# Scores of the causal and gated attention layers from rounded parts in fp32r, and the second sequence's causal layer moved beside the first biased layer

## The chip, the cores and the metric

The kernel runs on one core of a Trainium2 chip. The time is the device time of one execution in microseconds (us), the median of several runs. The engines are TensorE (PE for its matmuls, PEld for its weight loads), VectorE (DVE), ScalarE (ACT), GpSimd (POOL) and SyncE (SP), which here issues the DMAs.

## What is computed

Eight sequences of 512 tokens and 256 features go through four layers, each a layer norm, an attention and a sum with the input. The causal layer (0) and the gated layers (1 and 3) have 16 heads of 16 features; the biased layer (2) has 16 heads of 64.

```python
x = x + attn_a(_layernorm(x), ...)   # causal: rope on Q and K, softmax(QK/4), triangle
x = x + ffn(_layernorm(x), ...)      # gated: the 256 tokens with the highest gate attend to each other
x = x + attn_b(_layernorm(x), ...)   # biased: relative bias added to the scores
x = x + ffn(_layernorm(x), ...)      # gated again
```

All of it is float32, and the selection by the gate's order means that small errors could swap tokens.

## The kernel before

The work is cut into steps, such as `c_p1` or `b_row`, each of which belongs to one sequence and one layer. The letters are c for causal, f for gated and b for biased. `whole()` lists the steps with what each needs and follows, `in_order()` puts them in one order by a table of numbers `PLACE` (with the costs `WORK` as the planner's view of when banks come free), and every engine then walks its part of this one order. Engines meet by semaphores. The 8 banks of PSUM are given out by the planner in the same order.

Biased layers follow one another in the order of sequences and make up the main line. Beside biased layer s run the gated layer 3 of sequence s-1, the causal layer of sequence s+1 and the gated layer 1 of sequence s+1, one after the other, since they share one stretch of memory (`side[0]`). One such round is called a cycle here. Causal layer 1 is an exception: it has a second stretch (`side[1]`, which the biased layers use later), runs together with causal layer 0 and gated layer 1 of sequence 0, and biased layer 0 waits for it.

The scores of the small heads are computed twice. Pass 1 (`c_p1`, `f_p1`) gives queries by keys, from which DVE takes each row's maximum. The maxima are turned by PE (`c_m`, `f_m`). Pass 2 (`c_p2`, `f_p2`) gives keys by queries with the maximum subtracted, ACT takes the exponential, and the result is the operand for the values (`c_va`, `c_vb`, `f_va`, `f_vb`). Four heads are handled at once, one in each quarter of PE's 128 rows: 32 rows per matmul, 16 of which carry the head. Of the other 16, one holds ones in K (`K1`, `K1f`) and, before pass 2, the maximum in Q (`Qz`, `Qzf`), so that the maximum is subtracted by the same matmul. A causal layer has four such groups of four heads (`n` = 0 to 3), each in three steps per pass (`q` = 0: tiles 0 and 1 in pass 1; 1: tile 2; 2: tile 3), with 1280 columns per head and pass. A gated layer has four groups, one step per pass, with 512 columns.

All these operands are fp32. The trace records an fp32 matmul as two matmul records, each with its weight load. An fp32r matmul (`pick` by `xn_hi`, `xn_lo` in the gather) has one record. Where PE would be idle for long by the planner's view, transposes of `ident` fill the place (L1341).

## Time and profile before

| | |
|---|---|
| time, median of 3 runs | 2104.51 us (2104.4 to 2105.33) |
| the profiled execution | 2105.06 us |
| its span in the trace | 2103.3 us |
| PE busy in the span | 97% |
| DVE, ACT, POOL busy | 70%, 53%, 29% |

The span is the time from the first to the last instruction in the trace; 1.8 us of the profiled execution lie around it. Busy shares are means over the whole program, so a start in which engines wait for each other is mixed with the long even part.

### The profile page before, as it was taken

What the parts mean: (1) busy time and instruction counts of PE and PEld (TensorE: products, weight loads), DVE (VectorE), ACT (ScalarE), POOL (GpSimd) and SP (SyncE); (2) the same over time, 40 slices, a digit from 0 to 9 for tenths busy, and PEclk for the clock granted to TensorE, in tenths of its full rate; (3) what the DMA queues carried; (4) which work ended last, traced back from release to release, by engine and by line L of the source; (5) the groups of instructions that cost most, each with busy time, mean ns of one, the idle gap of its engine ahead of it and who ended that gap; (6) DMA issues with size and microseconds to landing.
All of it is one profiled execution on the core that took longest, in us unless ns stands there. A gap on an engine that the chain in (4) does not pass through costs nothing.

```text
span 2103.3 us, 38722 instructions
## 1 busy us (share of the span) xinstructions
PE 2029.9 (97%) x14644; PEld 1243.3 (59%) x14644; DVE 1467.4 (70%) x4578; ACT 1110.2 (53%) x2497; POOL 600.8 (29%) x817
## 2 busy tenths in 40 slices
PE   7889999999999999999999999999999999999997
PEld 4456556655665555765566645666456654666565
DVE  8887654777757766678767687576875777866435
ACT  1444664746537474464734646365563656535642
POOL 4212132243222342233411423124231243212220
PEclk9999999999999999999999999999999999999998
DMA  3001121121111110111101111012100121111200
GB/s 143 2 1 41 43 76 58 50 81 34 44 41 57 57 44 26 48 67 48 42 21 58 58 47 44 18 59 71 46 31 27 51 73 49 44 34 51 76 3 11
DMA packets 29047, 98.56 MB, mean 47 GB/s; under 512 B 2880, under 2 KB 11200, under 8 KB 28736
## 3 DMA queue, kind: packets, MB, share of 16 engines
q1 hardware_dynamic: 28864, 96.09, 13.6%
q8 instruction: 118, 1.93, 0.4%
q14 instruction: 65, 0.53, 0.1%
HBM read 91.89 MB, written 4.19 MB: 46 GB/s over the span
## 4 chain that ended last, share of the span: by engine, by line
PE 85%; DVE 7%; ACT 6%; issue 1%; POOL 0%; DMA 0%; SPq 0%; DVEq 0%; ACTq 0%; POOLq 0%
PE ps L861 26%; PE ps L1532 11%; PE ps L1550 10%; PE ps L1322 9%; PE ps L1540 9%; PE ps L1379 4%; PE ps L1488 3%; PE ps L1399 3%; PE ps L1500 3%; PE ps L1469 3%; PE ps L1413 2%; ACT PTc L1057 2%; ACT PT L1097 2%; DVE ps L1176 2%; DVE mcol L1251 1%; ACT probs L1088 1%
## 5 line engine op out<-in xcount | busy, mean ns | idle before, releaser
L1015 POOL TENSOR_SCALAR probs<-probs,rtotal 128x512 f32<-128x512 f32 x512 | 344.9, 693 | 871.8 <-DVE rtotal L1277 871.3
L1088 ACT ACTIVATE probs<-probs,peak 128x512 f32<-128x512 f32 x512 | 365.0, 714 | 220.9 <-DVE peak L1273 220.9
L1268 DVE CUSTOM_DVE_ANT_0 probs<-ps,band 128x512 f32<-128x512 f32 x512 | 332.6, 687 | 107.8 <-PE ps L1532 106.4
L1097 ACT ACTIVATE PT<-ps 128x512 f32<-128x512 f32 x512 | 263.1, 619 | 78.1 <-PE ps L1540 77.9
L1176 DVE CUSTOM_DVE_ANT_0 ps<-ps,later 128x128 f32<-128x128 f32 (+3 forms) x512 | 233.3, 525 | 40.9 <-PE ps L1379 40.0
L1540 PEld LDWEIGHTS ps<-ident,probs 128*128 128x128 f32 x2048 | 223.3, 141 | 52.0 <-issue 43.3
L1532 PE MATMUL ps<-KT,QT 64*128 64x512 f32 x1024 | 252.4, 611 | 0.0
L1540 PE MATMUL ps<-ident,probs 128*128 128x128 f32 x2048 | 248.3, 275 | 0.1
L1550 PE MATMUL ps<-PT,Vb 128*64 128x512 f32 x1024 | 235.9, 600 | 0.1
L861 PE MATMUL ps<-xnT,wb 128*128 128x512 f32 x512 | 233.0, 598 | 1.3 <-ACT PT L1097 0.7
L1057 ACT ACTIVATE PTc<-ps 128x384 f32<-128x384 f32 (+1 forms) x384 | 167.7, 542 | 64.8 <-PE ps L1399 64.7
L1251 DVE TENSOR_REDUCE mcol<-ps 128x2 f32<-128x512 f32 x256 | 157.3, 683 | 14.8 <-PE ps L1469 14.0
L1068 ACT ACTIVATE PTf<-ps 128x512 f32<-128x512 f32 x256 | 131.7, 604 | 63.0 <-PE ps L1488 62.6
L861 PEld LDWEIGHTS ps<-xnT,wb 128*128 128x128 f32 x512 | 92.9, 190 | 102.0 <-issue 96.8
L1532 PEld LDWEIGHTS ps<-KT,QT 64*128 64x128 f32 x1024 | 94.5, 186 | 92.9 <-issue 67.9
L1550 PEld LDWEIGHTS ps<-PT,Vb 128*64 128x64 f32 x1024 | 67.1, 137 | 139.2 <-issue 121.8
L861 PEld LDWEIGHTS ps<-wb,xnT 128*128 128x128 f32 x1024 | 122.6, 192 | 26.5 <-issue 16.7
L1007 POOL TENSOR_SCALAR_AFFINE_SELECT PTc<-PTc 128x512 f32<-128x512 f32 x128 | 82.1, 654 | 178.0 <-ACT PTc L1057 177.3
L983 POOL TENSOR_TENSOR rstd<-veps,pow_half 128x2 f32<-128x2 f32 x64 | 47.0, 737 | 280.8 <-DVE veps L1118 280.8
L861 PE MATMUL ps<-wb,xnT 128*128 128x128 f32 x1024 | 125.7, 276 | 0.0
L1322 PE MATMUL ps<-wob,OTb 128*128 128x256 f32 x512 | 114.0, 380 | 0.8 <-DVE OTb L1279 0.8
L1379 PE MATMUL ps<-K,Qz 32*128 32x128 f32 (+3 forms) x1024 | 96.5, 471 | 14.8 <-ACT PTc L1057 4.9
(133 smaller groups left out, 2887.3 us busy)
## 6 DMA issues: line engine op xcount, KB each, us to landing
band<-in_band SPq DMA_DIRECT2D x64, 896.0 KB, 4.6
wb<-in_w_b SPq DMA_DIRECT2D x64, 384.0 KB, 3.0
x<-in_x SPq DMA_DIRECT2D x16, 256.0 KB, 2.9
out<-x SPq DMA_DIRECT2D x16, 256.0 KB, 2.2
wob<-in_wo_b SPq DMA_DIRECT2D x1, 1024.0 KB, 8.7
wqk<-in_wqk_a SPq DMA_DIRECT2D x1, 512.0 KB, 6.2
cos_t<-in_cos SPq DMA_DIRECT2D x1, 256.0 KB, 5.4
sin_t<-in_sin SPq DMA_DIRECT2D x1, 256.0 KB, 6.5
```

Source lines behind the costliest of these rows:

```text
L861: last = nc.tensor.matmul(o, w, r, start=(i == 0), stop=(i == len(pairs) - 1))
L1015: last = g.tensor_scalar(unit, unit, rtotal[:, r % 8, e:e + 1], 1.0, ALU.mult, ALU.mult)
L1057: a.activation(pt_c(m, q)[:, h], bank(now, name)[:, 0:w], ACT.Exp).then_inc(act_read, 1)
L1088: last = a.activation(unit, unit, ACT.Exp, bias=peak[:, r % 8, e:e + 1], accum_out=total[:, r % 8, e:e + 1])
L1097: a.activation(PT[:, k % 2, e, :, tile_of(q)], bank(now, name).rearrange("p (k n) -> p k n", k=NT), ACT.Copy).then_inc(act_read, 1)
L1176: last = v.tensor_tensor_reduce(out=scores, in0=scores, in1=later[:, NT * P - w:NT * P], scale=1.0, scalar=-3e38, op0=ALU.add, op1=ALU.max ...
L1268: v.tensor_tensor_reduce(out=probs[:, r % ROWS_HELD, e, :], in0=bank(now, name), in1=band[:, k % 2, e, lo:lo + T], scale=1.0, scalar=-3e38 ...
L1322: last = te.matmul(o[:, j * D:(j + 1) * D], w, r, start=(k == 0 and j == 0), stop=(k == count - 1 and j == 1))
L1379: last = te.matmul(o[h][:, at_:at_ + w], m.Qz[group(h), c, e, tile_of(t)], m.K1[group(h), c, e, 0:w], start=True, stop=True)
L1532: full(te.matmul(bank(now, name), QT2[half(e), k % 2, tile_of(q)], KT2[half(e), k % 2, :], start=True, stop=True), now, name)
L1540: last = te.transpose(bank(now, name)[:, tile_of(t)], probs[:, r % ROWS_HELD, e, tile_of(t)], ident[:])
L1550: last = te.matmul(o[half(e), :], Vb[:, k % 3, q, half(e)], PT[:, k % 2, e, q, :], start=(q == 0), stop=(q == NT - 1))
```

## The change

The scores come from rounded fp32r parts. K is copied to both halves of the 32 rows and split into `HI` (rounded) and `LO` (the rest). Q is copied to both halves too, and `X` holds the rounded Q in one half and the rest in the other. `X` times `LO` plus `X` times `HI` is then the whole product of Q and K in two fp32r matmuls in place of one fp32 matmul. In pass 2 a third fp32r matmul subtracts the maximum: `M` (the turned maxima, themselves split in two by `c_hm` and `f_hm`) by `sel`. The scale 1/4 moves into the exponential. New steps make the parts: `c_dq`, `c_rq`, `c_xq`, `c_dk`, `c_hk` in a causal layer, `f_rq`, `f_xq`, `f_hk` in a gated one. They take the place of `c_hq` and the old `c_hk`, and `c_m`, `f_m` lose their DVE part to a copy on ACT.

The memory of the parts leaves no second stretch for a causal layer, so causal layer 1 follows gated layer 1 of sequence 0 and uses `side[0]`. The table `PLACE` and the costs `WORK` are new throughout.

```diff
@@ causal_steps, ffn_steps
-        out += [(c("q", i), [c("xt")], []), (c("k", i), [c("xt")], []), (c("hq", i), [c("q", i)], []),
-                (c("hk", i), [c("k", i)], [])]
+        out += [(c("q", i), [c("xt")], []), (c("k", i), [c("xt")], []), (c("dq", i), [c("q", i)], []),
+                (c("rq", i), [c("dq", i)], []), (c("xq", i), [c("rq", i)], []), (c("dk", i), [c("k", i)], []),
+                (c("hk", i), [c("dk", i)], [])]
+    out += [(f("rq"), [f("q")], []), (f("xq"), [f("rq")], []), (f("hk"), [f("k")], [])]
@@ whole
-    causal = [add(causal_steps(s), [], []) for s in range(2)]
-    entered = [add(ffn_steps(0, 1), causal[0], [])]
-    side = add(ffn_steps(1, 1), causal[1], entered[0])
+    entered = [add(ffn_steps(0, 1), add(causal_steps(0), [], []), [])]
+    side = add(ffn_steps(1, 1), add(causal_steps(1), [], entered[0]), [])
...
-        if s == 0:
-            layer = [(x, a, b + causal[1] * (x.kind == "b_k" and x.n == 0)) for x, a, b in layer]
@@ POOL
+                        if kind in ("c_hk", "f_hk"):
...
+                                last = g.tensor_tensor(low, both, high, ALU.subtract)
@@ ACT
+                        if kind == "c_rq":
...
+                            for e in range(2):
+                                last = a.activation(m.X[:, n, e], m.Dq[:, n, e], ACT.Copy, scale=sides[:, 0:1])
+                        if kind in ("c_m", "f_m"):
...
+                            a.activation(parts, bank(now) if kind == "c_m" else bank(now)[:, 0:CAP],
+                        if kind == "c_hk":
...
+                                a.activation(m.HI[:, n, e], m.LOf[:, n, e], ACT.Copy).then_inc(high_k_done, 1)
@@ DVE
+                        if kind in ("c_dq", "c_dk"):
...
+                                last = v.stream_shuffle(pairs[:, n, e], turned, [DH * e + r % DH for r in range(32)])
+                        if kind in ("c_xq", "f_xq"):
...
+                                last = v.scalar_tensor_tensor(out=parts, in0=both, scalar=sides[:, 1:2], in1=parts,
-                        if kind in ("c_m", "f_m"):
...
-                                last = v.scalar_tensor_tensor(out=rows[e], in0=peaks, scalar=sides[:, 6 + e:7 + e],
@@ PE, c_p1 (f_p1 alike)
-                                for h in range(4):
-                                    last = te.matmul(o[h][:, at_:at_ + w], m.Qz[group(h), c, e, tile_of(t)],
-                                                     m.K1[group(h), c, e, 0:w], start=True, stop=True)
+                                for some in (m.LO, m.HI):
+                                    for h in range(4):
+                                        last = te.matmul(o[h][:, at_:at_ + w], m.X[group(h), c, e, tile_of(t)],
+                                                         some[group(h), c, e, 0:w], start=(some is m.LO), stop=(some is m.HI))
@@ PE, c_p2 (f_p2 alike)
+                                for i in range(3):
+                                    for h in range(4):
+                                        one = sel[group(h), e:e + 1].to_broadcast([32, P])
+                                        w_ = (m.LO[group(h), c, e, tile_of(t)], m.HI[group(h), c, e, tile_of(t)], one)[i]
+                                        r_ = m.M[c][group(h), t * P:T] if i == 2 else m.X[group(h), c, e, t * P:T]
```

Of the table a line or two, as it stands everywhere:

```diff
-CYCLE = 2805
+CYCLE = 24741
-    ("cycle", "c_p1"): [-6358, 1818, 1797, -1735, 1672, 1720, 1843, 1993, 2033, 2063, 2084, 2140],
```

What this does to the order is seen on PE at the start of the program. Before, the second sequence's transposes of `xn` and its projections (`xnTc_103`) stand between the first sequence's projections (`xnTc_99`) and scores (`Qz_96`, `K_97`):

```order
L1341 MATMUL ps<-ident 128x128 x6
L861 MATMUL ps<-xnTc_99,wqk 128x512 x6
L1352 MATMUL ps<-ident,xn 128x128 x8
L861 MATMUL ps<-xnTc_99,wqk 128x512 x2
L861 MATMUL ps<-xnTc_103,wqk 128x512 x2
L1379 MATMUL ps<-K_97,Qz_96 128x128 x4
L1379 MATMUL ps<-K_97,Qz_96 128x256 x4
L861 MATMUL ps<-wva,xnTc_103 128x256 x4
```

Now only one sequence is at work there, all its projections come first, and transposes of `ident` fill the place before its scores:

```order
L1455 MATMUL ps<-ident 128x128 x6
L940 MATMUL ps<-xnTc_108,wqk 128x512 x8
L940 MATMUL ps<-wva,xnTc_108 128x256 x8
L1455 MATMUL ps<-ident 128x128 x29
L1494 MATMUL ps<-LO_102,X_98 128x128 x4
L1494 MATMUL ps<-HI_100,X_98 128x128 x4
L1494 MATMUL ps<-LO_102,X_98 128x256 x4
L1494 MATMUL ps<-HI_100,X_98 128x256 x4
```

Each block of four score matmuls has become two. The other place is PE where biased layer 0 begins (`xnT,wb` are its projections, `KT,QT` its scores). Before, gated layer 1 of sequence 1 starts beside it (`gate_80`), its causal layer having ended just ahead (`woa,Qz_100`):

```order
L1322 MATMUL ps<-woa,Qz_100 128x256 x8
L1341 MATMUL ps<-ident 128x128 x13
L1352 MATMUL ps<-ident,xn 128x128 x8
L1341 MATMUL ps<-ident 128x128 x6
L861 MATMUL ps<-xnT,wb 128x512 x6
L861 MATMUL ps<-wb,xnT 128x128 x8
L1426 MATMUL ps<-ident,gate_80 128x128 x4
```

Now the causal layer of sequence 1 begins here (the second transposes of `xn`, then `xnTc_108,wqk`) and its scores stand among the biased ones:

```order
L1466 MATMUL ps<-ident,xn 128x128 x8
L940 MATMUL ps<-xnTc_108,wqk 128x512 x8
L940 MATMUL ps<-xnT,wb 128x512 x4
L940 MATMUL ps<-wb,xnT 128x128 x8
L940 MATMUL ps<-xnT,wb 128x512 x4
L940 MATMUL ps<-wb,xnT 128x128 x8
L940 MATMUL ps<-wva,xnTc_108 128x256 x4
L1656 MATMUL ps<-KT_89,QT_88 128x512 x12
L940 MATMUL ps<-xnT,wb 128x512 x4
L940 MATMUL ps<-wb,xnT 128x128 x8
L1494 MATMUL ps<-LO_102,X_98 128x128 x4
```

The whole causal layer of sequence 1 has moved past the start of biased layer 0. The third place is DVE in the first gated layer. Before, K's parts are made in one step from PSUM (the ISA rows are a row maximum and its result):

```order
L1176 ISA ps,mcol_104<-ps,later 128x256
L1176 ISA mcol_104 128x1
L1240 TENSOR_SCALAR K1f_107<-ps,sides 128x512 x2
L1176 ISA ps,mcol_104<-ps,later 128x512
L1176 ISA mcol_104 128x1
```

Now DVE copies K (`gLOf`) and Q (`gDq`), and finishes `gX` after ACT has rounded it:

```order
L1354 TENSOR_SCALAR spread_t_126<-ps,slot_col 128x512 x2
L1281 STREAM_SHUFFLE gLOf_112<-ps 128x512 x2
L1281 STREAM_SHUFFLE gDq_114<-ps 128x512 x2
L1358 COPY Vx<-ps 128x32x16
L1275 SCALAR_TENSOR_TENSOR gX_109<-gDq_114,sides,gX_109 128x512 x2
L1365 TENSOR_REDUCE peaks<-ps 128x2 x8
```

No maxima of the other causal layer stand between these rows now. Counted over the whole order, PE changes its shape of tile (whole array, quarters of rows, halves, quarters of columns) 740 times before and 767 times now, and the transposes of `ident` between the gated layer and the next biased layer (x6 in each cycle) are gone.

## Rows read from the trace of the kernel before

**Rows 1.** The page, by engine: busy us, share of the span, instructions.

```profile
PE 2029.9 (97%) x14644; PEld 1243.3 (59%) x14644; DVE 1467.4 (70%) x4578; ACT 1110.2 (53%) x2497; POOL 600.8 (29%) x817
```

**Rows 2.** Windows, one cycle: length, busy us by engine (instructions), clock, DMA share, GB/s.

```profile
1094.92:1348.13 253.21, 249.08 (x1807) 151.24 (x1806) 182.34 (x572) 138.91 (x312) 74.56 (x100) 1.00 0.14 47
```

**Rows 3.** PE timeline, output projections of biased layers 6, 7: start us, length us.

```profile
1854.37 0.81 PE L1322 MATMUL ps<-wob,OTb 128*128 128x256 f32 x3
...
2032.66 1.56 PE L1322 MATMUL ps<-wob,OTb 128*128 128x256 f32 x6 [0.79 <-DVE OTb L1279]
```

**Rows 4.** PE timeline around 1005 us, columns as in rows 3.

```profile
1003.70 0.93 PE L1379 MATMUL ps<-K,Qz 32*128 32x384 f32 x8
1004.56 1.97 PE L1540 MATMUL ps<-ident,probs 128*128 128x128 f32 x16
1006.62 1.14 PE L1379 MATMUL ps<-K,Qz 32*128 32x512 f32 x8
1007.69 2.84 PE L1540 MATMUL ps<-ident,probs 128*128 128x128 f32 x24
1010.46 0.94 PE L1399 MATMUL ps<-Qz,K 32*128 32x256 f32 x16
```

**Rows 5.** PE timeline, the gather of the first gated layer (fp32r).

```profile
113.40 0.28 PE L861 MATMUL ps<-pick,xn_hi 128*128 128x256 f32 x1
...
114.95 0.28 PE L861 MATMUL ps<-pick,xn_lo 128*128 128x256 f32 x1
```

**Rows 6.** Weight-load timeline, two score steps of rows 4.

```profile
1006.59 0.34 PEld L1379 LDWEIGHTS ps<-K,Qz 32*128 32x128 f32 x8 [0.30 <-ACT PT L1097]
...
1010.46 0.74 PEld L1399 LDWEIGHTS ps<-Qz,K 32*128 32x128 f32 x16 [0.17 <-ACT PT L1097]
```

**Rows 7.** Groups on PE in the cycle of rows 2: busy us, mean ns.

```profile
L1399 PE MATMUL ps<-Qz,K 32*128 32x512 f32 (+3 forms) x128 | 11.9, 463 | 1.3 <-ACT PTc L1057 1.0
L1379 PE MATMUL ps<-K,Qz 32*128 32x256 f32 (+3 forms) x128 | 11.8, 463 | 0.4 <-DVE mcol L1176 0.3
L1413 PE MATMUL ps<-PTc,Vx 128*32 128x512 f32 (+3 forms) x128 | 10.5, 439 | 0.0
...
L861 PE MATMUL ps<-xnTc,wqk 128*128 128x512 f32 x16 | 7.3, 599 | 0.4 <-ACT xnTc L1040 0.4
...
L861 PE MATMUL ps<-wva,xnTc 128*128 128x256 f32 x16 | 3.9, 386 | 0.0
...
L1322 PE MATMUL ps<-woa,Qz 128*128 128x256 f32 x16 | 3.7, 386 | 0.0
```

**Rows 8.** PE timeline of the start of the program.

```profile
91.25 3.72 PE L1322 MATMUL ps<-woa,Qz 128*128 128x256 f32 x16 [0.55 <-DVE Qz L1206]
...
105.38 0.65 PE L1426 MATMUL ps<-ident,gate 128*128 128x128 f32 x4 [2.69 <-DVE gate L1211]
...
170.28 0.50 PE L1322 MATMUL ps<-of_hi,spread_t 128*128 128x256 f32 x2 [0.61 <-DVE of_lo L1282]
...
179.15 1.13 PE L861 MATMUL ps<-xnT,wb 128*128 128x512 f32 x2 [0.30 <-ACT xnT L1040]
```

**Rows 9.** PE timeline of the last gated layer.

```profile
2046.58 3.98 PE L1341 MATMUL ps<-ident 128*128 128x128 f32 x35
2052.48 0.65 PE L1426 MATMUL ps<-ident,gate 128*128 128x128 f32 x4 [1.92 <-DVE gate L1211]
...
2097.57 0.51 PE L1322 MATMUL ps<-of_hi,spread_t 128*128 128x256 f32 x2 [0.61 <-DVE of_lo L1282]
```

**Rows 10.** Groups by shape over the program: busy us, mean ns of one.

```profile
L993 POOL TENSOR_TENSOR xn_lo<-xn,xn_hi 128x512 fp32r<-128x512 f32 x32 | 40.1, 1275 | 62.1 <-ACT xn_hi L1033 62.1
...
L1184 DVE SCALAR_TENSOR_TENSOR Qz<-ps,sides,Qz 128x512 f32<-128x512 f32 x32 | 22.4, 741 | 0.9 <-PE ps L1389 0.9
...
L1159 DVE STREAM_SHUFFLE K<-ps 128x512 f32<-128x512 f32 x16 | 11.8, 736 | 0.0
...
L1033 ACT ACTIVATE xn_hi<-xn 128x512 fp32r<-128x512 f32 x32 | 18.2, 614 | 0.0
```

750 lines of the change are left out of this document (429 added, 321 removed).

## The prediction

> **What bounds the kernel now.** I read the page first, for which engine could bind. TensorE (PE) is busy in 97% of the span, the next engine in 70% [rows 1]. Then the PE timeline for the period: between the output projections of successive biased layers lie 253.2 us, and in one such cycle PE is busy 249.1 of 253.2 us at full clock, DVE 182.3, ACT 138.9, POOL 74.6 [rows 2]. So in six cycles PE's queue sets the time, and PE work taken out there is worth its length as long as the others keep up. From projection 6 to 7 it takes 178.3 us [rows 3], without a causal layer and one of the two gated ones: causal plus gated are worth 74.9 us of PE. The start is different. The first biased projection runs at 179.15 us [rows 8], and ahead of it PE waits for maxima, exponentials and gates. There, removing PE work is worth nothing and the length of the chain counts. The end (last gated layer alone) is such a chain too [rows 9].
>
> **PE, the scores, before.** Two pass-1 steps alone between other work: the 384-column one takes 0.86 us to the next start, the 512-column one 1.07 [rows 4]. The difference is 0.21 us for 128 columns, 1.65 ns a column, and what is left over is 0.22 us for the change of tile shape. A group of four heads has 1280 columns in each pass: 2.11 us of streaming. A gated group has 512 columns a pass: 0.845 us.
>
> **PE, the scores, after.** The trace has fp32r matmuls, on the whole array: from one of 256 columns to the next, 13 matmuls take 1.55 us, 0.12 us each, with their weight loads [rows 5]. That is 0.47 ns a column. An exact quarter of fp32's 1.65 would be 0.41, which I take as the other end. A matmul of 128 columns can't come faster than its weight load: transposes of 128 columns come each 0.115 us (24 in 2.77 us) [rows 4], so I take 0.11 as floor for a block of four quarters. At 0.47:
> - pass 1 of a causal group: 2 x (0.11 + 0.12) + 2 x 0.18 + 2 x 0.24 = 1.30 in place of 2.11;
> - pass 2, three matmuls for one: 0.72 + 0.54 + 3 x (0.11 + 0.12) = 1.95 in place of 2.11;
> - gated: 4 x 0.12 = 0.48 and 6 x 0.12 = 0.72 in place of 0.845 each.
>
> With four groups a layer that saves 3.9 us per causal and 2.0 per gated layer. At 0.41 (and 0.11 for 256 columns too) it is 5.2 and 2.4. I take 4.6 and 2.2, nearer the middle, since four small blocks may hide some of the gap between matmuls. The changes of shape stay (740 before, 767 now): 27 more at about 0.11 us, 3 us.
>
> The Trainium skill (TensorE: Matmul & The Clock Gate, LDWEIGHTS) gives a load 107 ns for 128 columns whatever the rows, which the trace's 0.115 us bears out. It also says there that a load overlaps running matmuls only in other row groups; I weigh that under the rivals.
>
> **The other engines.** Causal layer: DVE gains 8 shuffles and 4 sums at 0.74 us and loses 4 sums for the maxima and 4 scalings of K of about the same length: +3 us. Gated: 4 shuffles and 2 sums in, 2 scalings and 4 half-length sums out: +1.5. POOL gains 4 subtractions of 1.275 us per causal and 2 per gated layer: +5.1 and +2.6. ACT gains four roundings at 0.61 and two copies per causal layer, +3.7, and 2 per gated layer [rows 10]. Per cycle DVE goes to 188, ACT to 147, POOL to 85 us, in a cycle of 244: 77%, 60%, 35% [rows 2]. They cost nothing there, with PE's 95% or more as cover. In a chain that nothing covers they cost: in the gated layer alone, Q now takes shuffles 1.5, ACT 1.3, DVE 1.4, against 1.3 on ACT only: +3 us.
>
> **The sequence moved: the start.** Causal layer 0's output projection starts at 91.25 us [rows 8]. I leave that: DVE no longer serves the other sequence, but the maxima of one sequence and then ACT's exponentials of the last two groups stay in series, and Q and K get longer. From there the gated layer ran mixed with causal layer 1. Alone, its price is in the tail: 5.9 us from the end of the biased projection to the gate's transposes (2046.6 to 2052.5), then 45.1 to the last projection (2097.6) [rows 9]. So: 91.25 + 3.7 (the projection [rows 8]) + 5.9 + 45.1 + 3 = 149.0, and then the 8.9 us which lie between this projection and the biased layer now (170.28 to 179.15 [rows 8]): 157.9. The start ends 21 us sooner.
>
> But the causal layer that filled it is still to be done, and now stands in PE's queue beside biased layer 0, where PE is full. Its PE work in a cycle: 11.9 + 11.8 + 10.5 + 7.3 + 3.9 + 3.7 [rows 7] and about 2.4 of transposes, 51.5 us. These busy times overlap by some 5%; I take 49. What covered it before was idle PE; that cover is gone.
>
> **The sum**, on the profiled span of 2103.3: start -21; causal layer 1 moved +49; score matmuls in PE-bound stretches, 7 causal layers x 4.6 and 14 gated x 2.2 (all but sequence 0's causal and first gated and the very last gated): -63; changes of shape +3; the last gated layer's longer chain +3; the cycle's six filling transposes (0.8 us, six times) -5. Together -34: 2069. The three runs' median lies 0.6 below the profiled execution, and 1.8 us lie around the span: 2070 us, 1.6% faster. The cycle becomes 253.2 - 4.6 - 4.4 - 0.8 + 0.4 = 243.8.
>
> **Rivals.**
> 1. *Quarter-array weight loads set the pace (slower).* Blocks of 27 to 30 ns per pair of load and matmul are what I assume. The loads of 8 pairs begin within 0.34 us less one load of 0.185, 22 ns apart, but those of 16 pairs 37 ns apart [rows 6], there perhaps held by streaming. Per pair at 37 ns: a causal group 0.59 + 0.32 + 0.43 + 0.64 + 0.48 + 0.89 = 3.35, saving 0.9; a gated one 1.48, saving 0.2. Then -63 becomes -38 and the time 2096. At 54 ns (16 pairs in the 0.86 us of a step) pass 2 costs more than before and the time is 2160. It decides at 39 ns: no gain. By the Trainium skill (the same section), load and stream in one row group would add up and the new steps would be slower than the old ones; the gather speaks against it, with 0.12 us for both in the same rows [rows 5]. Chance 0.12.
> 2. *The side chain sets the cycle.* Gated, causal and gated layer follow one another in `side[0]` in each cycle. Unmixed they take 56.7 (the tail from 2046.6 to the end), 95 and 56.7: 208 us. With the longer Q and K about 220 of a cycle of 244. DVE's queue mixes the biased layer's maxima into it, so 24 us of slack may not do. Price: each microsecond that the cycle keeps costs 6. At a cycle of 247 the time is 2089, at 249.3 it is no change, at 253 slower by 1% (2125). For it: PE still waited in each cycle and had six filling transposes; against it: these are gone from the new order. Chance 0.16, a third of it beyond no change.
> 3. *More is gained.* The even stretch loses its waits (4.1 us of a cycle [rows 2]) and streaming is 0.41: cycle 240, time 2045. Chance 0.1.
> 4. *The start doesn't shorten.* Alone, the first sequence leaves PE at half clock and everything waits. Then +15: 2085. It is within the forecast's range; I count it there.
>
> **How the numbers follow.** The forecast (2055 to 2088) has 0.62, more by rival 3 0.10, rival 1 0.12 (half of it beyond no change), rival 2 0.16. The range reaches down to rival 3 and up to the milder ends of rivals 1 and 2: 2043 to 2103. Within 0.2% (4 us) is about what a measurement can't tell from no change. Faster: 0.62 + 0.10 + 0.05 + 0.09 = 0.86 less a little for what I don't see, 0.84. Same: 0.05. Slower: 0.11.
>
> **What would show it in the changed kernel's profile.** The starts of output projections of biased layers 2 to 6 should be 244 us apart; over 249 means rival 2 or 1. Pass-1 steps of 512 columns alone should take 0.70 us to the next start, gated pass-2 steps about 0.95; if 1.3, rival 1. The first biased projection should start near 158 us. DVE should be busy about 75% of the span, and PE still 96% or more. If PE's share falls to 94% with DVE or ACT as releasers, rival 2 has happened. The prediction is wrong if the start takes as long as before, or if the cycle's fall isn't the sum of its score steps' fall.

## The result

The changed kernel takes 2112.95 us (median of 6 runs, 2106.36 to 2113.5), the kernel before 2103.77 beside it: the ratio is 1.0036, with a 95% interval of 1.0026 to 1.0047. The forecast was 2070 us and faster; the kernel is slower by 0.4%. The profiled execution took 2113.5 us, with a span of 2111.8.

The page of the changed kernel by engine, the granted clock of TensorE over the span in 40 slices, and the chain that ended last:

```profile
PE 1989.5 (94%) x15710; PEld 1264.7 (60%) x15710; DVE 1543.4 (73%) x4834; ACT 1162.5 (55%) x2610; POOL 688.6 (33%) x879
...
PEclk7889999999999999999999999999999999999998
...
PE 65%; DVE 22%; ACT 6%; POOL 3%; issue 2%; DVEq 0%
```

TensorE works 40 us less than in [rows 1], and the span is 8 us longer. Its share is 94%, not 96. The chain runs over DVE for 22% of the span, where it was 7% before.

The windows between the starts of the output projections of biased layers 0 to 6, columns as in [rows 2]; the last line sums the six:

```profile
356.95:606.85 249.90, 240.90 (x1930) 151.84 (x1929) 192.33 (x604) 145.21 (x326) 85.86 (x108) 0.99 0.15 48
606.85:858.91 252.06, 242.66 (x1929) 151.56 (x1928) 192.47 (x604) 145.27 (x326) 85.79 (x108) 0.99 0.14 47
...
sum 1507.72, PE 1453.52 PEld 912.05 DVE 1154.56 ACT 872.00 POOL 515.06; mean PE 242.25 PEld 152.01 DVE 192.43 ACT 145.33 POOL 85.84
```

The cycle is 251.3 us on average, where 243.8 was forecast and [rows 2] has 253.2. Two things are to be seen. TensorE is busy 242.25 us of it, 9.0 less than the cycle, while in [rows 2] it is 4.1 less. And the clock is 0.99. Every cycle before had 1.00.

The chain of waits, TensorE's own, in the same six cycles (us in total, times, longest):

```profile
PE ps L1494 <- DVE peaks L1291: 13.2, 18, 1.3
PE ps L1589 <- DVE Vx L1358: 9.3, 6, 1.5
PE ps L940 <- DVE above L1340: 7.9, 6, 1.3
PE ps L1494 <- DVE X L1275: 6.5, 12, 0.9
PE ps L1518 <- ACT PTc L1163: 3.2, 12, 0.3
```

L1494 and L1589 are the first passes over the scores, causal and gated. TensorE's waits come to 8.6 us per cycle on the timeline (3.1 before), and most of the new ones end with DVE by the profile.

One of them has nothing to do with the added instructions. Before the comparisons `above` of a gated layer, GpSimd subtracts `xn_lo`; neither is new. In the kernel before GpSimd was done when they began. GpSimd first, then DVE:

```profile
1301.65 2.51 POOL L993 TENSOR_TENSOR xn_lo<-xn,xn_hi 128x512 fp32r<-128x512 f32 x2 [4.21 <-ACT xn_hi L1033]
```

```profile
1305.55 0.34 DVE L1221 TENSOR_SCALAR above<-gate_row,gate 128x256 bf16<-128x256 f32 x1
```

In the changed kernel they meet, and a comparison of 256 columns takes 1.37 us in place of 0.34:

```profile
1314.62 2.66 POOL L1068 TENSOR_TENSOR xn_lo<-xn,xn_hi 128x512 fp32r<-128x512 f32 x2 [6.39 <-ACT xn_hi L1117]
```

```profile
1314.78 1.37 DVE L1340 TENSOR_SCALAR above<-gate_row,gate 128x256 bf16<-128x256 f32 x1
1316.07 1.36 DVE L1343 TENSOR_SCALAR above<-gate_row,gate 128x256 bf16<-128x256 f32 x1
```

Two comparisons in each of the six cycles are so long, and the wait behind them, 1.31 us each time, makes the 7.9 us of L940. Every run below with the changed kernel's order in the cycle has it unchanged, also those with less side work. No run removes it alone.

One of the waits put down to the maxima, on TensorE's timeline (start, length, tile, wait ahead of it):

```profile
503.19 0.41 PE L1518 MATMUL ps<-M,sel 32*128 32x512 f32 x4
504.91 0.45 PE L1494 MATMUL ps<-LO,X 32*128 32x384 f32 x4 [1.31 <-DVE peaks L1291]
505.16 0.37 PE L1494 MATMUL ps<-HI,X 32*128 32x384 f32 x4
505.46 1.09 PE L1664 MATMUL ps<-ident,probs 128*128 128x128 f32 x8
506.81 0.59 PE L1518 MATMUL ps<-X,LO 32*128 32x384 f32 x4 [0.26 <-ACT PT L1199]
507.14 0.59 PE L1518 MATMUL ps<-X,HI 32*128 32x384 f32 x4
507.46 0.59 PE L1518 MATMUL ps<-M,sel 32*128 32x384 f32 x4
507.96 0.48 PE L1494 MATMUL ps<-LO,X 32*128 32x128 f32 x4
```

and the granted clock there, by windows of TensorE alone:

```profile
502.00:505.00 3.00, 1.60 (x32) 1.00 0.41 131
505.00:506.00 1.00, 1.00 (x13) 1.00 0.00 0
506.00:507.00 1.00, 0.74 (x10) 0.98 0.00 0
507.00:508.00 1.00, 1.00 (x16) 0.50 0.00 0
508.00:509.00 1.00, 1.00 (x19) 0.50 0.07 16
509.00:510.00 1.00, 1.00 (x8) 0.50 0.00 0
```

TensorE waits 1.31 us ahead of 504.91, and from 507 to 510 the clock is 0.50, the lower of its two levels (1.2 GHz). The blocks of 384 columns show it: 0.59 us long and 0.32 between starts at 507.14, and 0.37 long at 505.16, still at full clock. The clock shows 11 such stretches (half-clock stretches from here on) in the six cycles, none before. Each costs about 1.6 us. All 11 begin within 2.1 us of the end of a wait of 1.3 or 1.5 us. But of the 18 waits of that length in the six cycles 7 are not followed by one, with the same instructions around them. The place of 504.91 three cycles later, and the clock behind it:

```profile
1258.11 0.45 PE L1494 MATMUL ps<-LO,X 32*128 32x384 f32 x4 [1.31 <-DVE peaks L1291]
```

```profile
1260.00:1262.00 2.00, 1.64 (x29) 1.00 0.00 0
```

So the wait comes first, and what decides whether the clock falls after it isn't shown.

The first pass of a gated layer, columns the same:

```profile
909.98 0.32 PE L1589 MATMUL ps<-gHI,gX 32*128 32x256 f32 x4
910.09 0.32 PE L1589 MATMUL ps<-gLO,gX 32*128 32x256 f32 x4
910.21 0.32 PE L1589 MATMUL ps<-gHI,gX 32*128 32x256 f32 x4
912.07 0.39 PE L1589 MATMUL ps<-gLO,gX 32*128 32x256 f32 x4 [1.54 <-DVE Vx L1358]
```

Four matmuls of 256 columns come every 0.11 to 0.12 us, as in [rows 5]. Then comes a wait of 1.54 us.

### The profile page after: what moved, and what is told of

It is laid out like the page before. It is cut to its first block, busy times and chain, and to the rows that moved or that the text cites. A ratio compares the mean times of both kernels' runs of the same rounds, so it can differ in the third digit from the quotient of the medians.

```text
span 2111.8 us, 41452 instructions
## 1 busy us (share of the span) xinstructions
PE 1989.5 (94%) x15710; PEld 1264.7 (60%) x15710; DVE 1543.4 (73%) x4834; ACT 1162.5 (55%) x2610; POOL 688.6 (33%) x879
## 4 chain that ended last, share of the span: by engine, by line
PE 65%; DVE 22%; ACT 6%; POOL 3%; issue 2%; DVEq 0%
PE ps L940 17%; PE ps L1436 9%; PE ps L1664 9%; PE ps L1674 8%; PE ps L1656 8%; DVE ps L1291 5%; DVE probs L1382 5%; PE ps L1518 3%; PE ps L1623 2%; ACT PTc L1163 2%; PE ps L1611 2%; PE ps L1532 2%; PE ps L1494 2%; PE ps L1589 2%; DVE peaks L1365 1%
## 5 line engine op out<-in xcount | busy, mean ns | idle before, releaser
L1099 POOL TENSOR_SCALAR probs<-probs,rtotal 128x512 f32<-128x512 f32 x512 | 352.0, 708 | 516.8 <-DVE rtotal L1391 516.7
L1664 PE MATMUL ps<-ident,probs 128*128 128x128 f32 x2048 | 253.1, 277 | 0.6
L1664 PEld LDWEIGHTS ps<-ident,probs 128*128 128x128 f32 x2048 | 227.7, 142 | 40.3 <-issue 30.3
L1291 DVE CUSTOM_DVE_ANT_0 ps<-ps,later 128x512 f32<-128x512 f32 (+3 forms) x512 | 233.4, 526 | 21.9 <-PE ps L1494 21.5
L940 PE MATMUL ps<-xnT,wb 128*128 128x512 f32 x512 | 238.8, 611 | 0.8 <-DVE peak L1382 0.5
L1365 DVE TENSOR_REDUCE peaks<-ps 128x2 f32<-128x512 f32 x256 | 157.0, 683 | 19.2 <-PE ps L1589 19.2
L940 PEld LDWEIGHTS ps<-xnT,wb 128*128 128x128 f32 x512 | 94.8, 192 | 117.3 <-issue 111.7
L940 PEld LDWEIGHTS ps<-wb,xnT 128*128 128x128 f32 x1024 | 121.8, 192 | 16.8 <-issue 10.4
L940 PE MATMUL ps<-wb,xnT 128*128 128x128 f32 x1024 | 127.1, 278 | 0.3
L1436 PEld LDWEIGHTS ps<-wob,OTb 128*128 128x128 f32 x512 | 96.2, 190 | 12.5
```

The costliest lines, as they stand in the source:

```text
L940: last = nc.tensor.matmul(o, w, r, start=(i == 0), stop=(i == len(pairs) - 1))
L1099: last = g.tensor_scalar(unit, unit, rtotal[:, r % 8, e:e + 1], 1.0, ALU.mult, ALU.mult)
L1291: last = v.tensor_tensor_reduce(out=scores, in0=scores, in1=later[:, NT * P - w:NT * P], scale=1.0, scalar=-3e38, op0=ALU.add, op1=ALU.max ...
L1365: v.tensor_reduce(places[:, h:h + 1].rearrange("p h t -> p (h t)"), bank(now, name).rearrange("p (t n) -> p t n", t=NS), AXIS.X, ALU.max). ...
L1436: last = te.matmul(o[:, j * D:(j + 1) * D], w, r, start=(k == 0 and j == 0), stop=(k == count - 1 and j == 1))
L1664: last = te.transpose(bank(now, name)[:, tile_of(t)], probs[:, r % ROWS_HELD, e, tile_of(t)], ident[:])
```

## The experiments

All numbers of a cycle are means over the six intervals between output projections of layers 0 to 6; "idle" is TensorE's waiting on its timeline; DVE and POOL are busy times; "half clock" counts the stretches at the lower level in the six cycles. These columns are of the profiled execution, the time is the median. The two can differ: the changed kernel's profiled execution is the slowest of six (2113.5), that with both cuts the fastest of four (2075.02, at a mean clock of 0.982; the other three 2082.92 to 2085.41 at 0.976 to 0.978). So a difference of two or three stretches between rows may be that of executions.

| kernel | time, us | ratio to before (95%) | cycle | idle | DVE | POOL | half clock |
|---|---|---|---|---|---|---|---|
| before | 2103.77 | | 252.7 | 3.1 | 181.3 | 74.3 | 0 |
| after | 2112.95 | 1.0036 (1.0026 to 1.0047) | 251.3 | 8.6 | 192.4 | 85.8 | 11 |
| sums of 4 columns | 2090.31 | 0.9935 (0.992 to 0.995) | 248.3 | 6.4 | 187.1 | 84.3 | 8 |
| no subtraction | 2085.39 | 0.9916 (0.9898 to 0.9934) | 247.6 | 7.0 | 190.2 | 76.9 | 4 |
| both cuts | 2083.1 | 0.991 (0.9893 to 0.9926) | 246.7 | 6.0 | 186.0 | 75.8 | 3 |
| two matmuls | 2088.74 | 0.9926 (0.9911 to 0.9941) | 247.8 | 9.6 | 192.3 | 85.6 | 7 |
| low part twice | 2126.79 | 1.0114 (1.0099 to 1.0129) | 252.6 | 8.0 | 192.6 | 85.7 | 3 |
| before, more DVE | 2149.9 | 1.0212 (1.0195 to 1.0229) | 257.8 | 7.0 | 189.9 | 74.5 | 4 |
| reordered | 2121.41 | 1.0084 (1.0069 to 1.0099) | 253.7 | 11.7 | 192.7 | 87.4 | 8 |
| costs alone | 2115.39 | 1.006 (1.0045 to 1.0075) | 252.0 | 8.6 | 192.2 | 85.7 | 9 |
| copies on ACT | 2108.48 | 1.0018 (1.0008 to 1.0028) | 250.1 | 8.2 | 185.5 | 85.9 | 7 |
| before, copies on ACT | 2105.88 | 1.0003 (0.9993 to 1.0012) | 253.3 | 3.9 | 175.3 | 74.3 | 0 |
| repeat in causal pass | 2120.27 | 1.007 (1.0054 to 1.0086) | 252.2 | 8.6 | 192.6 | 85.9 | 5 |
| copies and repeat | 2123.04 | 1.0082 (1.0064 to 1.01) | 251.9 | 8.4 | 185.7 | 85.7 | 5 |
| signal per half | 2101.69 | 0.9987 (0.9978 to 0.9996) | 249.4 | 7.2 | 192.2 | 85.4 | 7 |
| signal and copies | 2095.06 | 0.9956 (0.9944 to 0.9969) | 248.0 | 6.5 | 185.3 | 85.5 | 5 |

### 1. Less side work

X's sums cut:

```diff
+                                few = slice(0, 4)
+                                both, parts = (both[:, few], parts[:, few]) if kind == "c_xq" else (both[:, 0, few], parts[:, 0, few])
                                 last = v.scalar_tensor_tensor(out=parts, in0=both, scalar=sides[:, 1:2], in1=parts,
```

> The changed kernel, with VectorE's eight sums per cycle that finish the operand X (scalar_tensor_tensor of 128x512, 1.05 us each in the changed kernel's trace) cut to 4 of the 512 columns; what is left out: X holds only one of its two parts in the other columns, so the scores are not the reference's. TensorE's instructions and the order of the steps stay. It takes some 7.6 us of 192.4 us per cycle from VectorE. Theory 1 (VectorE's queue makes TensorE wait: 8 to 10 us idle per cycle after, 3 before): the idle time falls to 4 to 5 us, the cycle from 251.3 to 246 or 247, the half-clock stretches with it, time 2075 to 2090. Theory 2 (the clock falls because the score steps are short, whoever is waited for): about as many half-clock stretches as the 11 of the changed kernel, cycle 249 or more, time 2098 or more. Theory 3 (what costs is the move of the second causal layer, not the cycle): within 5 us of 2113.

The time fell by 1.0% against the changed kernel, 23 us, just above theory 1's 2090; the cycle is 248.3. Theory 1 holds in direction; the idle time fell less than it said (6.4, not 4 to 5), and 8 half-clock stretches stayed.

LO's subtraction cut:

```diff
-                                    both, high, low = m.LOf[:, n, e], m.HI[:, n, e], m.LO[:, n, e]
+                                    both, high, low = m.LOf[:, n, e, 0:4], m.HI[:, n, e, 0:4], m.LO[:, n, e, 0:4]
...
```

> The changed kernel, with GpSimd's subtractions that make LO (1.31 to 1.37 us each, eight per cycle) cut to 4 columns and HI read in LO's place by TensorE at the same cost; what is left out: the low half of K, so the scores are rounded. Theory 1 (VectorE's own instructions fill its queue): the cycle falls by 1.5 us at most, time 2103 to 2113. Rival (VectorE and GpSimd slow each other: VectorE's comparison 'above' took 730 ns in the changed kernel beside these subtractions and 343 ns before; TensorE waited 7.9 us in six cycles for it): the comparison is back at about 340 ns, GpSimd's busy time per cycle falls from 85.8 to about 76, the cycle falls by 3 us or more and the time to 2095 or less.

The rival holds in time and cycle: 28 us, more than for the sums. But the comparison `above` of 256 columns stayed at 728 ns in the mean of 16, and so did TensorE's 7.9 us of waiting for it: what it meets is the subtraction for `xn_lo`, which this run leaves whole. What changed is X's sum. Both engines in the changed kernel, at one place of a gated layer, DVE and then GpSimd:

```profile
905.99 2.43 DVE L1275 SCALAR_TENSOR_TENSOR gX<-gDq,sides,gX 128x512 fp32r<-128x512 f32 x2 [0.22 <-ACT gX L1144]
908.34 0.68 DVE L1382 CUSTOM_DVE_ANT_0 probs<-ps,band 128x512 f32<-128x512 f32 x1
```

```profile
906.56 2.99 POOL L1084 TENSOR_TENSOR gLO<-gLOf,gHI 128x512 fp32r<-128x512 f32 x2 [2.75 <-ACT gHI L1153]
```

Two sums take 2.43 us while GpSimd subtracts, and its two subtractions take 2.99, where [rows 10] has 1.275 for one. At another place of the changed kernel, with GpSimd idle, two sums take 1.41 us, as at the same place with the subtraction cut:

```profile
1004.25 1.41 DVE L1275 SCALAR_TENSOR_TENSOR X<-Dq,sides,X 128x512 fp32r<-128x512 f32 x2
```

And the kernel without the subtraction, DVE:

```profile
892.93 1.41 DVE L1275 SCALAR_TENSOR_TENSOR gX<-gDq,sides,gX 128x512 fp32r<-128x512 f32 x2 [0.24 <-ACT gX L1144]
```

So a sum costs 0.74 us alone, which is what the prediction took, and up to 1.76 beside GpSimd (the mean of 32 is 1.05). Both are longer where they meet, each in its turn. The Trainium skill has the reason (SBUF — State Buffer, 🔬 SBUF: two separate sides): VectorE with two inputs in SBUF and a GpSimd instruction that reads SBUF exclude each other for a whole instruction. By that rule the sums were the ones to look at; the trace agrees.

Both cuts:

> The changed kernel with both cuts: X's sums and LO's subtractions on 4 columns each, HI read in LO's place (both left out of the scores as in the two single runs). The single cuts took 3.0 us (sums) and 3.7 us (subtractions) off the cycle of 251.3. If added side work is the whole miss of the forecast and its parts add: the cycle is 244 to 245.5, TensorE idle 4 to 5.5 us per cycle, at most 4 half-clock stretches, time 2060 to 2073, about the 2070 forecast. Rival (the two cuts remove the same waits; another wait, on the maxima or on the exponentials in PTc, stands behind): cycle 246.5 or more, idle 6 us or more, time 2077 to 2086.

The windows of the six cycles, the first and the sum:

```profile
349.30:595.24 245.94, 239.35 (x1930) 150.25 (x1929) 186.01 (x604) 144.94 (x326) 75.77 (x108) 1.00 0.15 48
...
sum 1480.33, PE 1441.71 PEld 906.21 DVE 1116.10 ACT 869.76 POOL 454.59; mean PE 240.28 PEld 151.04 DVE 186.02 ACT 144.96 POOL 75.76
```

The cycle is 246.7 and the time 2083.1, so the rival: the two don't add (3.0 and 3.7 us of the cycle alone, 4.6 together in the profiled executions; in the medians 23 and 28 us alone, 30 together). At full clock and without a half-clock stretch it is 246.0, with 239.35 of TensorE's work. That is the forecast's work (249.1 less 9.4 is 239.7). What stays are 6.0 us of waits a cycle. Of the 36 us in six cycles 15.4 end with ScalarE's exponentials `PTc` (4.7 in the changed kernel) and 7.9 still with `above`.

### 2. More or less of TensorE's work

The third matmul of pass 2 left out (`for i in range(2)`):

> The changed kernel, with the third matmul of each block of the second pass left out (the one that subtracts the maximum; the exponentials are of the raw scores), and nothing else. It takes 5 to 5.5 us of TensorE's occupied time per cycle. If TensorE's own work still set the cycle, it would fall by that to 246 and the time to about 2077. Theory 1 (waits on VectorE set it in these stretches): half or more of it turns up as idle time of TensorE (from 8-10 us per cycle to 11 or more), the cycle falls by 1 to 3 us, time 2093 to 2107. If short score steps lower the clock (theory 2), there are more half-clock stretches than 11 in six cycles, and the time may not fall at all.

The cycle is 3.5 us shorter, between the two answers (theory 1 had 1 to 3, TensorE's work alone 5). Cycle less idle fell from 242.7 to 238.2 us, some 1.1 of it by fewer half-clock stretches, so the matmuls were worth 3.4 and not 5. Only 1.0 us came back as waiting, not half. So of the 3.4 some seven tenths came off the cycle: TensorE's work still counts, if not in full. Theory 2 had more half-clock stretches with shorter steps, and there were fewer.

The opposite, the low part issued twice in pass 1 (`for i, some in enumerate((m.LO, m.LO, m.HI))`):

> The changed kernel with the low part's matmul of the first pass issued twice (the score is twice the low part plus the high part; nothing else differs): by the profile's 0.12 us for four of 256 columns some 5 us more of TensorE's occupied time per cycle, all in the first pass, where its four banks are read by VectorE in 2.4 us and written in about 1.3. Theory 1 (VectorE sets these stretches): 2 to 4 us of it fall into the waits, the idle time falls from 8.6 to 5 or 6 us per cycle, the half-clock stretches do not rise, cycle 252.5 to 254.5, time 2120 to 2132. If TensorE's work sets the cycle: cycle 256 to 257, time 2142 or more.

The place shown above for the changed kernel, and the same place two cycles later, on TensorE's timeline (the low part's block has 8 matmuls now, not 4):

```profile
510.30 0.62 PE L1494 MATMUL ps<-LO,X 32*128 32x384 f32 x8 [1.31 <-DVE peaks L1291]
...
1015.40 1.01 PE L1494 MATMUL ps<-LO,X 32*128 32x384 f32 x8 [1.31 <-DVE peaks L1291]
```

and the clock behind each:

```profile
510.00:513.00 3.00, 2.44 (x32) 1.00 0.00 0
514.00:516.00 2.00, 2.00 (x30) 1.00 0.03 8
...
1016.00:1017.00 1.00, 1.00 (x14) 0.50 0.06 16
```

The wait is 1.31 us both times, as in the changed kernel. The clock stays full at the first place and falls at the second. Over the six cycles 3 stretches are left, all three at this place. The cycle (252.6) and the time lie in theory 1's range, but not by its mechanism: the idle time was to fall to 5 or 6 us and is 8.0, and what kept the cycle short is the 8 stretches fewer. The undisturbed cycle is 252.2, some 4 longer than the changed kernel's would be (249.9, with one stretch, less 1.6), for 4.3 us more work. So the waits did not take up the added work. They behave like delays of fixed length and not like a pace that VectorE sets.

In the causal pass alone, with the result unchanged:

```diff
+                                for h in range(4):
+                                    te.matmul(o[h][:, at_:at_ + w], m.X[group(h), c, e, tile_of(t)],
+                                              m.HI[group(h), c, e, 0:w], start=True, stop=True)
                                 for some in (m.LO, m.HI):
```

> The changed kernel, complete, with one more matmul for each tile of the causal first pass, a repeat whose result the next one overwrites (some 3.5 us of TensorE's work per cycle; nothing else, and the gated layers as they are). If the half-clock stretches come from TensorE doing little in the causal score stretches: at most 3 of them in six cycles instead of 11, and as VectorE sets these stretches the cycle is 249.5 to 251, time 2105 to 2112: more work at no loss or a small gain. If the clock falls for another reason: 8 or more stretches, cycle 252.5 to 254, time 2120 or more.

5 stretches instead of 11, and the cycle 0.9 us longer: neither answer in full. The one cycle without a stretch is 250.8, 2.5 more than the changed kernel's would be, for 2.5 us more work. The filling costs more than the clock gives back. None of the 5 stretches stands in the causal pass, and four follow the wait for Vx in the gated layer, where nothing was added.

### 3. The same load in the kernel before

```diff
+                            for i in range(2):
+                                v.stream_shuffle(swapped, bank(now), [r ^ 1 for r in range(32)]).then_inc(extra_done, 1)
+                                extra[0] += 1
+                                dve.wait_ge(extra_done, extra[0])
                             v.stream_shuffle(swapped, bank(now), [r ^ 1 for r in range(32)])
```

and two more scalings for `f_k`, written alike.

> The kernel before, with extra work on VectorE alone: each shuffle of a causal projection is made three times and each scaling of the gated keys twice, in the same tiles with the same values, some 9 to 10 us per cycle on its 182.3 us, about what the change added. TensorE's work, order and scores are before's, and the output stays the reference's. Theory 1: TensorE's idle time rises by 3 to 6 us per cycle, the cycle from 253.2 to 256 or 258, time 2122 to 2140. Rival (VectorE's 70 idle us per cycle hide it; what costs in the changed kernel is the order or the clock): cycle within 1 us of 253.2, time 2104 to 2112.

The sum over its six cycles:

```profile
sum 1546.49, PE 1499.75 PEld 906.32 DVE 1139.48 ACT 832.80 POOL 446.85; mean PE 249.96 PEld 151.05 DVE 189.91 ACT 138.80 POOL 74.48
```

The cycle rose by 5.1 us, as theory 1 had it, and the time by 45, more than it had; 14 of the 45 came before the first output projection (352.2, before 338.2). Half-clock stretches appear in the kernel before too, so they don't need the short score steps; four of its six waits of 3.0 us are followed by one. Where TensorE waits tells more, in the same six cycles:

```profile
PE ps L1391 <- issue: 18.1, 6, 3.0
```

L1391 is the first pass of the causal layer. These six waits are 18.1 of the 23 us that were added, one in each cycle, ahead of the first scores behind the lengthened chain. (The profile names no engine for them; at 729.56 TensorE starts 0.10 us after DVE's last scaling of K.) That speaks for lateness and against load, and part 5 tests it in the changed kernel.

### 4. Order and move

The costs in the planner's table (the reordered kernel has new rows in its table of places as well):

```diff
-    "c_dq": [("dve", 0.65), ("dve", 0.65)],
...
+    "c_dq": [("dve", 0.74), ("dve", 0.74)],
...
-    "c_xq": [("dve2", 0.66), ("dve2", 0.66)],
...
+    "c_xq": [("dve2", 1.05), ("dve2", 1.05)],
...
```

> The changed kernel with the planner's cost table set to what the changed kernel's trace measured (X's sum 1.05 us instead of 0.66, shuffles 0.74 instead of 0.65, rounding on ScalarE 0.71 and 0.62 instead of 0.65 and 0.55, GpSimd's subtraction 1.32 instead of 1.26, M's copies 0.64 and 0.39 instead of 0.5 and 0.3), and the whole table of places searched again with these costs. Every instruction is the changed kernel's; only their order and the banks differ. Theory 1a (the waits came from an order made for durations that the chip does not have): TensorE's idle time per cycle falls from 8.6 to 6 us or less, the half-clock stretches from 11 to 6 or fewer, cycle 247 to 249, time 2092 to 2103. Theory 1b (the 10 us of added VectorE work cannot be hidden by any order of these steps): cycle 250.5 or more, time 2106 to 2116.

> The changed kernel with the measured costs in the planner's cost table and its table of places left as it is: the order of the steps is the same, and only the choice of PSUM banks, which goes by modelled times, differs. The kernel reordered with these costs had cycles of 253.7 us, and 11.8 us idle per cycle. Theory 2a (the order was what made that one worse): here cycle 250.5 to 252, time 2109 to 2116. Theory 2b (the banks did): cycle 253 or more, time 2120 or more. Theory 2c (the banks of the changed kernel were chosen by wrong durations and cost it waits): cycle 249.5 or less, time 2103 or less.

The reordered kernel is slower than the changed one, by a cycle of 253.7 with 11.7 us idle; with the same costs and the old table the cycle is 252.0, so it was the order (2a). In the new order the comparisons `above` are short again, and yet TensorE waits 13.1 us in six cycles for them, 2.19 us each time. No order found with one number per instruction was better. Why is argued only: a sum is 0.74 or 1.76 us by its neighbour, a comparison 0.34 or 1.37, which a table with one number can't say.

The changed kernel without the move (and the kernel before with it, by the same lines the other way round):

```diff
-    entered = [add(ffn_steps(0, 1), add(causal_steps(0), [], []), [])]
-    side = add(ffn_steps(1, 1), add(causal_steps(1), [], entered[0]), [])
+    causal = [add(causal_steps(s), [], []) for s in range(2)]
+    entered = [add(ffn_steps(0, 1), causal[0], [])]
+    side = add(ffn_steps(1, 1), causal[1], entered[0])
...
```

> The changed kernel without the move: scores from exact parts, but the second sequence's causal layer stands beside the first one again, in the second memory, ahead of the biased layer of sequence 0. The rows of the table for the start (first, first0, first1) are searched anew for this order with the planner's own costs; the rows of the cycle and the tail are the changed kernel's, word for word. Theory A (the move costs: it starts sequence 0's biased layer 26.6 us earlier and makes it 45.4 us longer, +19): the first output projection is at 335 to 345 us instead of 356.95, the cycles stay at 251.3, time 2093 to 2102. Theory B (the move is neutral; TensorE is so full in the start that the layer costs the same in either place): first output projection at 352 to 362, time 2108 to 2118.

> The kernel before with the move alone: its own scores, but sequence 1's causal layer after sequence 1's turn comes, beside the biased layer of sequence 0; the rows of the table for the start are searched anew with its own costs, those of the cycle and the tail are before's. Theory A (the move costs 19 us net at the start): first output projection at 352 to 362 us instead of 338.20, cycles 253.2, time 2118 to 2128. If the move pays by itself (the start's idle time of TensorE, 45 us in the changed kernel's first 152, is what it removes): 2095 or less. Theory B (neutral): 2100 to 2110.

> The kernel with the scores alone (no move), its rows for the start searched longer and with the measured costs; the rows of the cycle and the tail are the changed kernel's, word for word. The first search left a second interval of 274.1 us between output projections where the changed kernel has 249.9. If that was the table and not the missing move: first output projection at 345 to 350 us, the second 246 to 251 later, cycles 251.3, time 2093 to 2103, which would beat both kernels. If a start without the move cannot be as short: the first two together at 610 or more, time 2112 or more.

> The two last edits together: scores alone (no move), with the measured costs and the whole table searched again. If the two effects add: the time of the reordered kernel less the gain (or plus the loss) that the kernel with the scores alone shows against the changed kernel; by theories A and 1a together 2075 to 2092, which would beat both kernels by more than 0.5%; by theories B and 1b 2106 to 2116.

| kernel | time, us | ratio (95%) | output projection of layer 0 at | of layer 1 at |
|---|---|---|---|---|
| before | 2103.77 | | 338.20 | 588.57 |
| after | 2112.95 | 1.0036 | 356.95 | 606.85 |
| scores alone | 2121.18 | 1.0083 (1.0066 to 1.0099) | 340.84 | 614.93 |
| scores alone, better start | 2117.2 | 1.0063 (1.0046 to 1.0081) | 359.27 | 607.84 |
| move alone | 2139.04 | 1.0162 (1.0146 to 1.0177) | 356.27 | 621.02 |
| scores alone, reordered | 2140.23 | 1.0166 (1.015 to 1.0182) | 354.05 | 614.32 |

("Better start" doesn't compute all of the reference; which part is not known, so I read only its lengths.) Move alone costs 32 us by the second projection; its first projection is where theory A had it, its time is above both theories. With the new scores the move gives 1 to 8. So theory A falls: without the move the first projection is early (340.84), as it said, but the second is not. By the second projection the kernels with the new scores are 18 to 26 us behind the kernel before, with or without the move. Each has its own searched table for the start, so how much of this is the scores' and how much the tables' isn't separated. The last row repeats that the reordered cycle is worse: 256.6.

### 5. Load or lateness

Copies of Q and of the gated values moved to ScalarE:

```diff
+                            a.activation(QT2[:, k % 2, :], bank(now), ACT.Copy,
+                                         scale=float(DB) ** -0.5).then_inc(act_read, 1)
...
-                            v.tensor_scalar(QT2[:, k % 2, :], bank(now), float(DB) ** -0.5, None,
-                                            ALU.mult).then_inc(dve_read, 1)
...
```

> The changed kernel, complete, with two kinds of copy out of PSUM moved from VectorE to ScalarE: the biased layers' Q (eight of about 0.6 us per cycle) and the gated layers' values (two of about 0.6). Order of the steps as in the changed kernel. About 6 us less on VectorE per cycle (192.4 to 186.4), 5 more on ScalarE (145 to 150). By the rate that two runs gave (5.4 us less VectorE work took 3.0 us off the changed kernel's cycle, 8.6 more put 4.6 to 5 us on before's) the cycle falls by 3.2 to 248, time 2088 to 2098, faster than before. Rival (only work ahead of X counts; these copies stand where VectorE has slack, or ScalarE's queue, which gives the exponentials, takes over the waits): cycle 250.5 or more, time 2107 or more.

> The kernel before with the same two kinds of copy on ScalarE. If VectorE's load only matters since the change (TensorE was idle 3.1 us per cycle before, and waited mostly for ScalarE's PTc): cycle 252.7 to 253.3, time 2100 to 2108. If it mattered before at the same rate: cycle 250 or less, time 2085 or less. If ScalarE's exponentials come later for it: cycle 254 or more, time 2112 or more.

> The two edits of the runs ahead together: copies on ScalarE and the repeated matmul in the causal first pass. If they add: the cycle is that of the copies alone less 0 to 1.5 us, with at most 3 half-clock stretches, time 2083 to 2096. If VectorE's relief lets TensorE run ahead so that it is TensorE's work that sets the cycle again, the repeat costs its 3.5 us: 10 to 20 us above the kernel with the copies alone.

6.9 us off DVE gave 1.2 of the cycle, a third of the rate that theory 1 had. Of that 0.4 is waiting; four half-clock stretches fewer make most of the rest, and a cycle without any is 248.4, against the 248.3 that the changed kernel's would be. The kernel before gained nothing. With the repeat it is 15 us slower than without, the second answer there: TensorE's work costs what it takes.

The same instructions in the same order, with each half of X (ScalarE's rounding and VectorE's sum) and of LO signalled when done:

```diff
-                                last = v.scalar_tensor_tensor(out=parts, in0=both, scalar=sides[:, 1:2], in1=parts,
-                                                              op0=ALU.mult, op1=ALU.add)
-                            last.then_inc(halves_q_done, 1)
+                                v.scalar_tensor_tensor(out=parts, in0=both, scalar=sides[:, 1:2], in1=parts,
+                                                       op0=ALU.mult, op1=ALU.add).then_inc(halves_q_done, 1)
...
-                            at_least(pe, halves_q_done, plan.after("halves_q", Step("c_xq", s, l, c), now))
+                            at_least(pe, halves_q_done, plan.after("halves_q", Step("c_xq", s, l, c), now) - 1 + e)
...
```

> The changed kernel, complete, with the same instructions in the same order; only the signals differ: each half of X (ScalarE's rounding, VectorE's sum) and of LO (GpSimd's subtraction) is announced when it is done instead of both together, so that TensorE's first pass over the first half can begin one sum (1.05 us) and one subtraction (1.31 us) earlier. Load theory (VectorE's busy time sets the waits): nothing changes, cycle 250.8 to 251.8, time 2109 to 2115. Lateness theory (TensorE runs out of work because X and LO are late): TensorE's waits for X, which were 6.5 + 2.5 us in six cycles, go, and some of those that the profile puts down to what VectorE did just before (maxima, Vx); cycle 249 to 250.3, time 2097 to 2107.

The chain of waits of TensorE in its six cycles:

```profile
PE ps L1492 <- ACT PTc L1162: 12.4, 12, 1.3
PE ps L940 <- DVE above L1338: 7.9, 6, 1.3
PE ps L1587 <- DVE Vx L1356: 7.4, 6, 1.3
PE ps L1492 <- DVE peaks L1289: 3.5, 10, 0.4
...
PE ps L1492 <- DVE X L1274: 1.2, 6, 0.2
```

Lateness, then, for the part that this edit reaches. DVE is as busy as in the changed kernel (192.2), and the time is 11 us less. At the same mean clock of an execution, 0.975, it is 2102.38 and 2102.68 against 2110.87, so some 8 us are not the clock's. The waits for X fell from 6.5 to 1.2 us. Those put down to the maxima fell from 13.2 to 3.5, but at the place of the 1.31 us wait one of 1.32 stays, now put down to ScalarE's exponentials, which took over 12.4: the profile names the last of several, and there the edit changed the name and not the wait. X's sums meet GpSimd less too: in the six cycles 6 of 48 take over 1.5 us, 12 in the changed kernel.

> The signals per half together with the copies of Q and of the gated values on ScalarE. The copies alone gave a cycle of 250.1 and 2108.5 us. Lateness theory, both adding: cycle 248 to 249.3, time 2093 to 2102, ahead of the kernel before. Load theory: as the copies alone, 2105 to 2112.

Its cycles, the second and the sum:

```profile
607.86:854.74 246.88, 239.74 (x1929) 150.55 (x1928) 185.38 (x594) 150.09 (x336) 85.56 (x108) 1.00 0.15 48
...
sum 1487.90, PE 1446.11 PEld 907.22 DVE 1111.88 ACT 900.87 POOL 513.17; mean PE 241.02 PEld 151.20 DVE 185.31 ACT 150.14 POOL 85.53
```

2095.06 us, 0.44% faster than the kernel before and 0.8% faster than the changed one, complete: the version that beats both.

## Why the prediction was wrong

The forecast was 43 us short, and the six cycles account for all of it. They take 1507.7 us; before they took 1516.2, and 6 x 9.4 less was forecast, 1459.8. That is 48 us. The start, the last interval (174.9 against 178.3 in [rows 3]) and the tail were right within 3 us each.

- **The score steps were right.** TensorE's work in an undisturbed cycle is 239.3 us against 249.1, 9.8 less; 9.4 was forecast. A block of four 256-column matmuls comes every 0.12 us at full clock. Rival 1 is refuted: the block pays the gather's price. The Trainium skill's sentence that it cited (TensorE: Matmul & The Clock Gate; it stands under The mechanism, not under LDWEIGHTS, and the text ahead of it also lets a load into the background weight buffer go ahead), read so that load and stream in one row group add up, doesn't hold here. The signs for the steps came: a first-pass step of 512 columns takes 0.66 us to the next start (0.70 forecast), a gated second-pass step 0.91 (0.95).
- **The step that failed** is "They cost nothing there, with PE's 95% or more as cover", of the other engines' added work. A busy share of 95% says that TensorE has work in its queue, not that the next one in the queue has its operands. The new chain behind a projection (shuffles, roundings, sums or subtractions) made X and LO late: gaps (cycle less TensorE's busy time) went from 4.1 to 9.0 us, +30 in six cycles. Half of that, 15.5 us, goes when the sums and subtractions are cut. Another 7.9 are the waits for `above`, which are no added work: two old instructions on DVE and GpSimd meet in the new order. The remaining 6 or so no run takes apart. Signalling per half took 11 us back with no work removed; this is shown. The prediction took all of this as covered and priced neither the place of the added work nor what the new order brings together.
- **The clock.** 18 of the 48 us are TensorE's own work at half clock, 242.25 instead of 239.3 per cycle. The forecast had full clock as in [rows 2] and no term for it. Shown: the stretches follow waits, and appear in the kernel before when it is made to wait. Fewer of them come with a fuller first pass (3 and 5), but not by place: one of those kernels keeps them just where the pass was filled. Not settled: why one wait of 1.3 us brings it and another, with the same instructions around it, doesn't.
- **Sizes.** X's sum was 0.74, and is 1.05 in the mean, by collisions with GpSimd: 8 x 0.31, 2.5 us of DVE per cycle. The two long comparisons add 2 us. DVE has 192.4 and not 188.
- **The start**: TensorE goes through without a pause from 150.4 us on; the first biased projection came at 162.1, behind the first ones of the moved layer, where 157.9 was forecast. The first output projection moved from 338.2 to 357.0, by 18.8, with 21 forecast (-21 + 49 less 7 for its scores). Rival 4's price didn't come, though its sign did in part: the granted clock up to 152.5 was 0.82 (0.96 up to 179.15 before).
- **Rival 2** was nearest: its mark (a cycle over 249, PE's share at 94%, DVE as releaser) is what came. Its price was right, 249.3 for no change and 6 us for each microsecond. Its chance was too small, because I weighed the length of the whole side chain, not how late each operand would be. That the whole chain sets the cycle isn't shown: work added to TensorE costs nine tenths of its length or all of it (low part twice, repeat).

## What to carry to other kernels

Where the busiest engine stands at 97% and its work is cut by 4%, price the chain that hands it its operands: each added instruction there can make its operand late by its length, and by that of what it collides with, however idle its engine is on average. After a new order, look for old instructions of VectorE and GpSimd that have come to overlap. Signal each part when it is done, and put the copies that anyone can do on the engine that isn't in that chain. Waits that a change brings can cost TensorE's clock as well; look at the granted clock of stretches, not of the span.

## What was not expected of the hardware

- A sum of two SBUF operands on VectorE takes 0.74 us alone and up to 1.76 beside a GpSimd subtraction, and the subtraction grows with it (2.99 for two, where [rows 10] has 1.275 for one). A comparison with one 256-column input and bf16 output grows too, from 0.34 to 1.37 us.
- Up to 2.1 us after a single wait of 1.31 or 1.54 us, in a kernel whose TensorE is busy 96% of the cycle, the granted clock went to half (11 times of 18). After the same wait among the same matmuls it also stayed full.
- Four matmuls of 32 rows and 256 columns in fp32r, with a weight load each, come every 0.12 us, no slower than one of 128 rows.
